# The order of TensorE's work inside a pair of heads, written out as a table: masks, V products and plain score tiles placed anew, VectorE's order with it

## The chip, the cores and the metric

One Trainium2 chip (trn2), one of its cores. The metric is the device time of one execution in microseconds (us): the median of three runs of the kernel before is 3874.01 us (3871.12 to 3876.84).

## The reference, cut to what matters

```python
x = L0_attn_x                                  # (8, 1024, 512) float32
xn = _layernorm(x)
qkv = xn @ W_attn + b_attn                     # q, k, v: 16 heads of 32
att = einsum('bhqd,bhkd->bhqk', q, k) * HD ** (-0.5)
att = where(causal, att, -inf);  att = softmax(att)
y = einsum('bhqk,bhkd->bhqd', att, v) @ W_proj + b_proj
x = x + y + ffn(xn)                            # ffn: SwiGLU, 512 -> 1408 -> 512, FP4-rounded operands
```

The change touches only the softmax attention of the eight batches. Projections and feed-forward stay as they are.

## The kernel before, in words

The kernel works through eight batches, seven in a loop and the last one written out behind it, and then the feed-forward part, 64 tiles of 128 rows. In a batch it projects q, k and v, then goes through the 16 heads in eight **pairs** (`p` = 0 to 7), then multiplies by the output weights. A pair is split into eight **units** `u`, one for each block `kt` of 128 keys.

TensorE does five kinds of work in a pair:

- **Plain score tiles**, `scores(p, n)` (L983): 128 queries against all keys up to them, used only for the row maximum. There are 16 in a pair of heads, n = 0 to 15. Tiles of even n have 640, 768, 896 and 1024 keys and go to the PSUM tile `ps_s`; those of odd n have 512, 384, 256 and 128 keys and go to `ps_dense`. `mask_scores` (L988) adds the causal mask, and VectorE takes the maximum (`row_max`, L609, the tile `mx`). A tile waits until VectorE has read the one two places ahead of it (`s_max`). Tile n stands one or two pairs ahead: the first `EARLY` tiles of pair 1 are made before pair 0 starts; beside pair p stand tiles `EARLY` to 15 of pair p+1, and then, after the maxima of p+1, the tiles 0 to `EARLY`-1 of pair p+2.
- **Maxima**, `maxima(p+1)` (L993): one transposition of all 16 maxima. It needs all 16 `row_max`. VectorE splits the result (`split_max`, L615 and L617), and SP's queue puts it into the stack of operands with two DMAs.
- **Transposed scores**, `transposed_scores(p, kt, i)` (L1010): parts of up to 512 queries; four parts in units 0 to 3 and two in units 4 to 7, 24 in all. They go through a ring of three PSUM banks, `ps_st`: a part waits until ScalarE has taken the exponential (L883) of the part three places ahead. A part on the diagonal gets `mask_transposed` (L1017) before ScalarE may read it.
- **V products**, `times_v(p, kt)` (L1029), four column tiles of 32 side by side: a **visit** here is an uninterrupted run of such narrow products.
- **Denominators**, `denominators(p)` (L1046), also narrow: ones times the sums that GpSimd makes of the exponentials of blocks 0 to 4 (`sum_up`, L536 to L541, tile `stage`), and times the exponentials of blocks 5 to 7 (in `rob`). They are made one pair late, and go to the bank that the odd score tiles use.

From the denominators a chain leads on: VectorE copies them out (`copy_den`, L626), SP's queue spreads them with four small DMAs (`den_rows`, L458), VectorE inverts them (`invert`, L630), SP's queue sends the inverse out and back (L463, L466), and VectorE divides the V product (`divide`, L646).

Every engine's order is fixed by the program. Queues on SP: `den_rows`, the two DMAs of the maxima, the spreading of the inverse, and then, in pairs 1 to 4 of a batch, seven DMAs (L409) that load the q and k of a pair three ahead; these go out as soon as the last exponential of the pair before is done. The storage of the exponentials of block 4 is also that of block 1, so ScalarE may write block 1 of the next pair only once GpSimd has added block 4.

## Time and profile before

| | |
|---|---|
| median of the runs | 3874.01 us |
| profiled execution | 3873.68 us, span of its core 3871.9 us |
| TensorE (PE) busy | 3745.3 us, 97% |
| VectorE (DVE) / ScalarE (ACT) / GpSimd (POOL) busy | 2628.4 / 1212.9 / 932.3 us |
| mean granted TensorE clock | 0.985 |
| attention | eight batches up to about 2320 us of the span, some 281 us each |
| the batch read here | projections from 1161 us, pair 0 at 1244.5, pair 6 at 1371.5, output product 1410.7 to 1442 us |

PE is nearly always busy by the profile, but busy time of pipelined matmuls covers small gaps; what an order costs is read from start to start. In the batch read here the eight pairs begin at 1244.48, 1265.92, 1287.0, 1308.19, 1329.28, 1350.4, 1371.47 and 1390.85 us.

### The profile page before, as it was taken

What the parts mean: (1) busy time and instruction counts of PE and PEld (TensorE: products, weight loads), DVE (VectorE), ACT (ScalarE), POOL (GpSimd) and SP (SyncE); (2) the same over time, 40 slices, a digit from 0 to 9 for tenths busy, and PEclk for the clock granted to TensorE, in tenths of its full rate; (3) what the DMA queues carried; (4) which work ended last, traced back from release to release, by engine and by line L of the source; (5) the groups of instructions that cost most, each with busy time, mean ns of one, the idle gap of its engine ahead of it and who ended that gap; (6) DMA issues with size and microseconds to landing.
All of it is one profiled execution on the core that took longest, in us unless ns stands there. A gap on an engine that the chain in (4) does not pass through costs nothing.

```text
span 3871.9 us, 63727 instructions
## 1 busy us (share of the span) xinstructions
PE 3745.3 (97%) x21836; PEld 2696.1 (70%) x21836; DVE 2628.4 (68%) x3834; ACT 1212.9 (31%) x2313; POOL 932.3 (24%) x462
## 2 busy tenths in 40 slices
PE   8999999999999999999999989999999999999999
PEld 6557556557557556556556548888888888888887
DVE  5665665665665666665666647777777777777777
ACT  2441441441442532532532522222222222222222
POOL 0550550550650641641641630000000000000000
PEclk9999999999999999999999999999999999999999
DMA  5425425426325335335236440111111111111110
GB/s 194 101 73 178 102 73 176 99 73 186 83 88 176 80 105 157 79 118 157 67 117 191 134 164 28 32 31 32 32 32 33 33 33 33 33 33 32 32 31 32
DMA packets 178222, 337.02 MB, mean 87 GB/s; under 512 B 42432, under 2 KB 50112, under 8 KB 176832
## 3 DMA queue, kind: packets, MB, share of 16 engines
q1 hardware_dynamic: 153504, 275.75, 25.1%
q10 hardware_dynamic: 24480, 58.21, 4.4%
q8 instruction: 135, 2.21, 0.3%
q14 instruction: 103, 0.84, 0.1%
HBM read 213.92 MB, written 118.43 MB: 86 GB/s over the span
## 4 chain that ended last, share of the span: by engine, by line
PE 91%; DVE 4%; issue 2%; ACT 1%; DMA 1%; SPq 0%; ACTq 0%; DVEq 0%; POOL 0%
PE f_ps L1471 25%; PE ps_dense L959 13%; PE f_ps_o L1483 12%; PE ps_st L1010 9%; PE ps_s L983 6%; PE ps_dense L1128 5%; PE ps_dense L1029 4%; PE ps_y L1029 4%; PE ps_dense L1046 3%; DVE mx L609 2%; PE ps_st L1017 2%; PE ps_dense L983 2%; PE f_ps L1463 1%; PE ps_s L988 1%; PE ps_st L928 1%
## 5 line engine op out<-in xcount | busy, mean ns | idle before, releaser
L1471 PE MATMUL f_ps<-wgu,xqt 128*128 128x512 f32 (+1 forms) x4608 | 992.6, 373 | 1.4 <-DVE xqt L1331 1.4
L1471 PEld LDWEIGHTS f_ps<-wgu,xqt 128*128 128x128 f32 x4608 | 842.2, 188 | 122.9 <-DVE xqt L1331 1.7
L883 ACT ACTIVATE pt<-ps_st 128x512 f32<-128x512 f32 (+3 forms) x1152 | 551.4, 527 | 656.5 <-PE ps_st L1017 508.5
L609 DVE TENSOR_REDUCE mx<-ps_s 128x1 f32<-128x640 f32 (+3 forms) x576 | 553.7, 961 | 200.6 <-PE ps_s L988 197.6
L541 POOL TENSOR_TENSOR stage<-stage,pt 128x1536 f32<-128x1536 f32 (+2 forms) x176 | 518.4, 2945 | 15.2
L1483 PE MATMUL f_ps_o<-wd,hqt 128*128 128x512 f32 x2112 | 510.9, 394 | 0.6 <-DVE hqt L1357 0.6
L539 POOL TENSOR_TENSOR stage<-pt 128x1792 f32<-128x1792 f32 x64 | 258.3, 4036 | 1012.0 <-ACT pt L883 1012.0
L1483 PEld LDWEIGHTS f_ps_o<-wd,hqt 128*128 128x128 f32 x2112 | 390.9, 188 | 78.9 <-DVE hqt L1357 0.8
L959 PE MATMUL ps_dense<-arena,wa 128*128 128x512 f32 x1536 | 391.7, 402 | 12.9 <-DVE stage L662 7.0
L609 DVE TENSOR_REDUCE mx<-ps_dense 128x1 f32<-128x512 f32 x448 | 219.2, 489 | 217.0 <-PE ps_dense L988 211.9
L959 PEld LDWEIGHTS ps_dense<-arena,wa 128*128 128x128 f32 x1536 | 281.2, 190 | 74.2 <-issue 10.6
L1010 PE MATMUL ps_st<-stack 98*128 98x512 f32 (+3 forms) x768 | 308.3, 425 | 0.2
L1010 PE MATMUL ps_st<-arena 98*128 98x512 f32 (+3 forms) x768 | 282.5, 409 | 3.4 <-ACT pt L883 1.3
L1017 PE MATMUL ps_st<-identb,causal 128*128 128x128 bf16 x1024 | 239.3, 234 | 0.0
L1010 PEld LDWEIGHTS ps_st<-stack 98*128 98x128 f32 x768 | 146.2, 199 | 127.3 <-ACT pt L883 68.6
L1010 PEld LDWEIGHTS ps_st<-arena 98*128 98x128 f32 x768 | 138.9, 190 | 137.2 <-ACT pt L883 75.6
L1128 PE MATMUL ps_dense<-wp,yt 128*128 128x512 f32 x512 | 229.2, 598 | 2.5 <-DVE rob L657 2.0
L1418 ACT ACTIVATE silu<-f_ps 128x512 f32<-128x512 f32 (+1 forms) x192 | 107.0, 557 | 370.5 <-PE f_ps L1471 370.5
L983 PE MATMUL ps_s<-stack 96*128 96x512 f32 (+1 forms) x576 | 181.1, 388 | 35.1 <-DVE mx L609 28.7
L848 ACT ACTIVATE stage<-ps_dense,bqk 128x512 fp32r<-128x512 f32 x128 | 87.5, 687 | 348.8 <-PE ps_dense L959 304.3
L959 PE MATMUL ps_dense<-wa,arena 128*128 128x512 f32 x768 | 189.9, 397 | 0.0
L1413 ACT ACTIVATE ha<-ht 128x1408 f32<-128x1408 f32 x63 | 87.0, 1382 | 325.2 <-DVE ht L1254 325.2
(130 smaller groups left out, 4876.1 us busy)
## 6 DMA issues: line engine op xcount, KB each, us to landing
qk_scratch<-stage SPq DMA_DIRECT2D x128, 512.0 KB, 2.9
stack<-qk_scratch SPq DMA_DIRECT2D x192, 256.0 KB
arena<-qk_scratch SPq DMA_DIRECT2D x192, 256.0 KB
xs<-in_L_attn_x SPq DMA_DIRECT2D x64, 256.0 KB, 3.8
rob<-in_L_attn_x ACTq DMA_DIRECT2D x64, 256.0 KB, 2.8
acc_scratch<-rob ACTq DMA_DIRECT2D x64, 256.0 KB, 2.1
xt<-in_L_attn_x SPq DMA_DIRECT2D x64, 256.0 KB, 2.6
at<-acc_scratch SPq DMA_DIRECT2D x64, 256.0 KB, 2.6
```

What stands on the lines that cost most here:

```text
L539: nc.gpsimd.tensor_tensor(both[:, :, cols], exps(0)[:, :, cols], exps(1), ALU.add).then_inc(summed_up, 1)
L541: nc.gpsimd.tensor_tensor(both[:, :, cols], both[:, :, cols], exps(kt), ALU.add).then_inc(summed_up, 1)
L609: nc.vector.tensor_reduce(mx[:, h * ST + q:h * ST + q + 1], scores_bank(p, n)[:, 0:(q + 1) * P], axis=AX.X, op=ALU.max, negate=True).then_ ...
L883: nc.scalar.activation(exps(kt)[:, h, q - kt * P:q - kt * P + n], ps_st[:, w % ST_RING, 0:n], ACT.Exp, scale=SCALE).then_inc(st_exp, 1)
L959: last = nc.tensor.matmul(bank(*use), left(lh, k), right(rh, k), start=n == 0, stop=n == len(terms) - 1)
L983: nc.tensor.matmul(out[:, k0:k1], qs, stack(p)[0:KS, 2 + h, k0:k1], start=True, stop=k1 < keys)
L1010: last = nc.tensor.matmul(ps_st[:, w % ST_RING, 0:n], stack(p)[0:KM, 2 + h, kt * P:(kt + 1) * P], stack(p)[0:KM, h, q:q + n], start=True, ...
L1017: nc.tensor.matmul(ps_st[:, w % ST_RING, 0:P], causal[:, :], identb[:, :], start=False, stop=True).then_inc(st_full, 1)
L1029: last = nc.tensor.matmul(by_tile(y_bank(p)[y_rows(h, s), y_cols(kt, s)]), v_head(kt, p, h), exps_of_parity(kt, h, s), start=kt == 0, stop ...
L1128: last = nc.tensor.matmul(bank("P", k), yt[:, g, t * P:(t + 1) * P], wp[:, g, :], start=g == 0, stop=g == G - 1)
L1471: last = nc.tensor.matmul(ps[:, SLOT[c], gu, 0:n].rearrange("p (j n) -> p j n", n=P), xqt[:, a, k], wgu[:, b, gu * FC + f // P:gu * FC + ( ...
L1483: last = nc.tensor.matmul(ps_o[:, :], hqt[:, a, k], wd[:, b, k], start=i == 0, stop=i == len(terms) - 1)
```

## The change

`SHARE`, `M_UNIT`, `DEN_UNIT` and `Y_UNIT` go. TensorE's order in a pair is read from a table with a row for each unit: `T` is the next plain score tile, `MT` the masks of all tiles that lack one, `S0` to `S3` the parts of transposed scores, `M0` to `M3` their masks (a `-` names the unit before), `P0` to `P7` the V products, `DEN` the denominators and `MAX` the maxima. VectorE has a table of its own. No instruction is added or removed on any engine but ScalarE's wait registers.

```diff
-    SHARE = [2, 3, 3, 2, 2, 2, 2, 0]
-    M_UNIT = 2
-    EARLY = TILES - sum(SHARE[:M_UNIT + 1])
-    DEN_UNIT = 1
-    Y_UNIT = ST - 1
+    STEPS = ["T MT S0 S1 T MT S2 T S3 MT M2 P5 T M3 MT DEN P6",
+             "S0 S1 S2 T MT T MT M2 S3 T MT M3 P7 P0 MAX",
+             "S0 T S1 S2 T MT M2 P1 T MT S3 M3",
+             "S0 T MT S1 S2 T MT M2 S3 T M3",
+             "S0 M0 MT S1",
+             "S0 T S1 T M1- MT M0 M1 P2 P3",
+             "S0 S1",
+             "S0 T MT M0- M1- M0 P4 S1 M1"]
+    VECTOR_STEPS = "R R R R DEN R R R MAX INV R R R R R R R Y R R"
+    FLAT = " ".join(STEPS).split()
+    EARLY = TILES - FLAT[:FLAT.index("MAX")].count("T")
...
@@ VectorE
-                    if p == PAIRS - 2 and not final and 0 <= u - M_UNIT - 1 < XR:
-                        stats(b + 1, u - M_UNIT - 1)
+                    elif step == "MAX":
+                        if p + 1 < PAIRS:
+                            split_max(p + 1)
+                        if p == PAIRS - 2 and not final:
+                            for t in range(XR):
+                                stats(b + 1, t)
...
@@ ScalarE
+                            act.wait_ge(pv_done, ONE + b * PAIRS * ST + p * ST)
...
@@ TensorE: of a pair
-                    elif 0 < u <= RINGED:
-                        times_v(p, u - 1)
+                        elif step[0] == "P":
+                            kt = int(step[1])
+                            if kt < u:
+                                times_v(p, kt)
+                            elif p:
+                                times_v(p - 1, kt)
```

`EARLY` goes from 8 to 9. P5, P6 and P7 of a pair are made in units 0 and 1 of the next one, P0 in unit 1, P1 in unit 2, P2 and P3 in unit 5, P4 in unit 7. Written in the same letters, the order before was:

```
u0: S0 S1 T S2 M2 MT P5 P6 P7 S3 T M3 MT
u1: S0 S1 T S2 M2 MT DEN P0 S3 T T M3 MT
u2: S0 T S1 T S2 M2 MT P1 S3 T M3 MT
u3: S0 S1 MAX T S2 M2 MT P2 S3 T M3 MT
u4: S0 T M0 MT P3 S1 T M1 MT
u5: S0 T M0 MT P4 S1 T M1 MT
u6: S0 T M0 MT S1 T M1 MT
u7: S0 M0 S1 M1
```

**Place A, TensorE, end of unit 1 and start of unit 2 of a middle pair, before.** The tiles of 896, 256 and 1024 keys (the last three rows on L983) follow each other with two parts between them.

```order
L983 MATMUL ps_s<-arena 128x384
L1017 MATMUL ps_st<-identb,causal 128x128
L988 MATMUL ps_dense<-causal,identb 128x128
L988 MATMUL ps_s<-causal,identb 128x128
L1008 REGISTER_ALU
L1010 MATMUL ps_st<-arena 128x512
L978 REGISTER_ALU
L983 MATMUL ps_dense<-arena 128x256
L1008 REGISTER_ALU
L1010 MATMUL ps_st<-arena 128x512
L978 REGISTER_ALU
L983 MATMUL ps_s<-arena 128x512 x2
```

The same three tile sizes after (now in units 0 and 1; the 896 tile stands ahead of the denominators, so the rows begin with the 256 tile): three parts go ahead of the 256 tile, and it and the 1024 tile have a mask between them.

```order
L1036 MATMUL ps_st<-arena 128x512
L1034 REGISTER_ALU
L1036 MATMUL ps_st<-arena 128x512
L1034 REGISTER_ALU
L1036 MATMUL ps_st<-arena 128x384
L1002 REGISTER_ALU
L1009 MATMUL ps_dense<-arena 128x256
L1014 MATMUL ps_dense<-causal,identb 128x128
L1004 REGISTER_ALU
L1009 MATMUL ps_s<-arena 128x512 x2
L1014 MATMUL ps_s<-causal,identb 128x128
L1043 MATMUL ps_st<-identb,causal 128x128
```

What moved: the tile of 256 keys comes a whole run of narrow products and three parts after the one of 896, which was one part before.

**Place B, TensorE, the denominators of the pair before; before the change.** They stood in unit 1, ahead of P0.

```order
L1017 MATMUL ps_st<-identb,causal 128x128
L988 MATMUL ps_s<-causal,identb 128x128
L1034 REGISTER_ALU
L1036 REGISTER_ALU
L1046 MATMUL ps_dense<-stage,ones 32x512 x4
L1046 MATMUL ps_dense<-rob,ones 32x128 x2
L1046 MATMUL ps_dense<-rob,ones 32x256 x2
L1046 MATMUL ps_dense<-rob,ones 32x128 x6
L1023 REGISTER_ALU
L1029 MATMUL ps_dense<-pt,v 32x512 x4
```

After: they end unit 0, behind the masks of the 896 tile, and P6 follows them.

```order
L1009 MATMUL ps_s<-arena 128x384
L1043 MATMUL ps_st<-identb,causal 128x128
L1014 MATMUL ps_s<-causal,identb 128x128
L1060 REGISTER_ALU
L1063 REGISTER_ALU
L1073 MATMUL ps_dense<-stage,ones 32x512 x4
L1073 MATMUL ps_dense<-rob,ones 32x128 x2
L1073 MATMUL ps_dense<-rob,ones 32x256 x2
L1073 MATMUL ps_dense<-rob,ones 32x128 x6
L1055 MATMUL ps_y<-rob,v 32x128 x4
```

What moved: `denominators` from behind three of unit 1's parts to ahead of all of them, and P6 from unit 0's one run of P5, P6 and P7 to behind it.

**Place C, VectorE, from the maxima on, before.** `inv` was inverted two row maxima after the split of the maxima.

```order
L615 CAST mr<-ps_dense 16x128
L617 TENSOR_TENSOR mr<-ps_dense,mr 16x128
L608 REGISTER_ALU
L609 TENSOR_REDUCE mx<-ps_s 128x1
L608 REGISTER_ALU
L609 TENSOR_REDUCE mx<-ps_dense 128x1
L629 REGISTER_ALU
L630 RECIPROCAL inv<-den 128x16
L608 REGISTER_ALU
```

After: at once behind the split.

```order
L633 REGISTER_ALU
L634 REGISTER_ALU
L635 CAST mr<-ps_dense 16x128
L637 TENSOR_TENSOR mr<-ps_dense,mr 16x128
L649 REGISTER_ALU
L650 RECIPROCAL inv<-den 128x16
L628 REGISTER_ALU
L629 TENSOR_REDUCE mx<-ps_s 128x1
L628 REGISTER_ALU
```

What moved: the reciprocal, past two row maxima. Since MAX itself moves from unit 3 to the end of unit 1, all row maxima of the pair's second half now stand behind the reciprocal.

## Rows read from the trace of the kernel before

**Rows 1.** Stretches: us; busy of PE, PEld, DVE, ACT, POOL; clock, DMA share, GB/s.
```profile
1308.19:1329.28 21.09, 20.39 (x171) 11.84 (x170) 14.46 (x23) 10.71 (x25) 13.26 (x6) 1.00 0.39 86
```

**Rows 2.** PE timeline, pair 3, units 1 and 2: start, us, instruction, idle before.
```profile
1316.38 0.48 PE L1010 MATMUL ps_st<-arena 98*128 98x512 f32 x1
1317.17 0.38 PE L983 MATMUL ps_dense<-stack 96*128 96x256 f32 x1 [0.31 <-DVE mx L609]
1317.39 0.39 PE L1010 MATMUL ps_st<-arena 98*128 98x512 f32 x1
1318.17 0.73 PE L983 MATMUL ps_s<-stack 96*128 96x512 f32 x2 [0.39 <-DVE mx L609]
```

**Rows 3.** PE timeline, pair 3, unit 4, and the passage to pair 4.
```profile
1323.18 0.22 PE L988 MATMUL ps_dense<-causal,identb 128*128 128x128 bf16 x1
1323.21 0.48 PE L1010 MATMUL ps_st<-arena 98*128 98x512 f32 x1
1323.53 0.51 PE L983 MATMUL ps_s<-stack 96*128 96x512 f32 x2
...
1329.08 0.23 PE L1017 MATMUL ps_st<-identb,causal 128*128 128x128 bf16 x1
1329.28 0.74 PE L1010 MATMUL ps_st<-stack 98*128 98x512 f32 x2
```

**Rows 4.** PE timeline, pair 3: denominators with P0, and P1.
```profile
1312.64 1.06 PE L1046 MATMUL ps_dense<-stage,ones 128*32 128x512 f32 x8
...
1315.36 0.44 PE L1010 MATMUL ps_st<-arena 98*128 98x384 f32 x1
...
1319.13 1.06 PE L1029 MATMUL ps_y<-pt,v 128*32 128x384 f32 x8
1320.13 0.38 PE L1010 MATMUL ps_st<-arena 98*128 98x256 f32 x1
```

**Rows 5.** DVE timeline, pair 3: denominators' copy, and the next division.
```profile
1314.69 0.69 DVE L626 COPY rob<-ps_dense 128x512 f32<-128x512 f32 x1 [0.98 <-PE ps_dense L1046]
...
1330.58 1.41 DVE L646 TENSOR_TENSOR yt<-ps_dense,rob 64x512 f32<-64x512 f32 x2 [0.62 <-DMA rob<-inv_scratch]
```

**Rows 6.** SP's issues, pair 3: q and k, denominators, inverse out.
```profile
1308.56 2.67 SPq L409 DMA_DIRECT2D arena<-qk_scratch  x6
...
1315.41 3.54 SPq L458 DMA_DIRECT2D den<-rob  x4
...
1324.32 0.34 SPq L463 DMA_DIRECT2D inv_scratch<-inv  x1
```

**Rows 7.** The tile `den` from 1308 to 1331 us.
```profile
DMA to landing us min/median/max: 1.7/2.6/3.1
```

**Rows 8.** Stretches around the end of the DMA traffic, pair 3.
```profile
1316.50:1318.00 1.50, 1.00 0.12 17
```

**Rows 9.** POOL and PE timelines, pairs 6 and 7.
```profile
1380.61 4.01 POOL L539 TENSOR_TENSOR stage<-pt 128x1792 f32<-128x1792 f32 x1 [7.77 <-ACT pt L883]
...
1385.27 8.93 POOL L541 TENSOR_TENSOR stage<-stage,pt 128x1536 f32<-128x1536 f32 x3
```

**Rows 10.** PE timeline, pairs 6 and 7: their first parts, both runs of denominators.
```profile
1371.47 0.73 PE L1010 MATMUL ps_st<-arena 98*128 98x512 f32 x2
...
1394.55 1.06 PE L1046 MATMUL ps_dense<-stage,ones 128*32 128x512 f32 x8
...
1407.41 0.62 PE L1046 MATMUL ps_s<-stage,ones 128*32 128x512 f32 x2
```

**Rows 11.** PE timeline, start of pair 0.
```profile
1244.48 1.20 PE L1010 MATMUL ps_st<-stack 98*128 98x512 f32 x2
1245.69 0.90 PE L983 MATMUL ps_s<-stack 96*128 96x512 f32 x2
```

**Rows 12.** A stretch of the early tiles of pair 1.
```profile
1242.00:1244.00 2.00, 1.27 (x4) 0.60 (x3) 1.30 (x2) 0.00 (x0) 0.00 (x0) 0.50 1.05 242
```

**Rows 13.** The page, part 5: feed-forward products of 512 columns: busy, mean ns.
```profile
L1471 PE MATMUL f_ps<-wgu,xqt 128*128 128x512 f32 (+1 forms) x4608 | 992.6, 373 | 1.4 <-DVE xqt L1331 1.4
```

More of the change, by code:

```diff
@@ L1078, in body @@
                 mask_scores(1, n)
+            due, unmasked = 0, []
             for p in range(PAIRS):
+                pe.wait_ge(m_in, ONE + b * PAIRS * 2 * DMA + (p + 1) * 2 * DMA)
                 for u in range(ST):
-                    tiles = beside(p, u)
-                    if u == 0:
-                        pe.wait_ge(m_in, ONE + b * PAIRS * 2 * DMA + (p + 1) * 2 * DMA)
-                    parts = len(PARTS[u])
-                    ahead = 2 if u == M_UNIT else 1
-                    for i in range(parts // 2):
-                        transposed_scores(p, u, i)
-                        if u == M_UNIT and i < ahead:
-                            for n in tiles[i:i + 1]:
-                                scores(*n)
@@ L1092, in body @@
-                    if u == M_UNIT + 1 and p + 1 < PAIRS:
-                        maxima(p + 1)
-                    if u != M_UNIT:
-                        for n in tiles[:ahead]:
-                            scores(*n)
-                    if parts > 2:
-                        transposed_scores(p, u, 2)
-                    mask_transposed(p, u, parts - 2)
-                    for n in tiles[:ahead]:
-                        mask_scores(*n)
-                    if u == DEN_UNIT and p:
-                        denominators(p - 1)
@@ L1104, in body @@
-                    if u == 0 and p:
-                        for kt in range(RINGED, ST):
-                            times_v(p - 1, kt)
-                    elif 0 < u <= RINGED:
-                        times_v(p, u - 1)
-                    transposed_scores(p, u, parts - 1)
-                    for n in tiles[ahead:]:
-                        scores(*n)
-                    mask_transposed(p, u, parts - 1)
-                    for n in tiles[ahead:]:
-                        mask_scores(*n)
@@ L1115, in body @@
-            for kt in range(RINGED, ST):
+                    for step in STEPS[u].split():
+                        if step[0] == "S":
+                            transposed_scores(p, u, int(step[1]))
+                        elif step[0] == "P":
[4 more added lines that the diff above has]
+                                times_v(p - 1, kt)
+                        elif step == "T":
+                            tile, due = tile_of(due), due + 1
+                            if tile[0] < PAIRS:
+                                scores(*tile)
+                                unmasked.append(tile)
+                        elif step == "MT":
+                            for tile in unmasked:
+                                mask_scores(*tile)
+                            unmasked = []
+                        elif step == "DEN":
+                            if p:
+                                denominators(p - 1)
+                        elif step == "MAX":
+                            if p + 1 < PAIRS:
+                                maxima(p + 1)
+                        else:
+                            mask_transposed(p, u - step.count("-"), int(step[1]))
@@ L1116, in body @@
+            for kt in PV_LATER:
                 times_v(PAIRS - 1, kt)
```

55 lines of the change are left out of this document (30 added, 25 removed).

## Prediction

> **What bounds the kernel now.** I read the busy shares first, then the pairs' starts, then TensorE's timeline of one middle pair from start to start, then what the other engines do at the same places. Pair 3 lasts 21.09 us, and TensorE is busy in 20.39 of them, at a granted clock of 1.00, 2.4 GHz; VectorE 14.46, ScalarE 10.71, GpSimd 13.26 [rows 1]. So TensorE's own order sets a middle pair, and its two true gaps, 0.31 and 0.39 us, make up the whole of the missing 0.70: both are plain score tiles that wait for VectorE's maximum [rows 2]. GpSimd, though it is busy for 13 us only, sets the passage from pair 6 to pair 7 (below), and the start of pair 0 runs at the lower clock.
>
> What the reader is to see in [rows 2]: the part S0 starts at 1316.38, and the next instruction, a tile of 256 keys, at 1317.17, 0.79 us later. The same succession without a wait takes 0.32 us (1323.21 to 1323.53) [rows 3]. The next part and the tile of 1024 keys behind it take 0.78 us again. Excess: 0.47 + 0.46 = 0.93 us. The tile behind the wait also starts with its weights not yet loaded: 256 columns take 0.22 us there. In an unbroken run a product of up to 512 columns takes 992.6 / 4608 = 0.215 us [rows 13], so 256 take some 0.11; I add 0.2 for both tiles. The waits cost 1.1 us a pair; bounds: the bare gaps, 0.70, and 1.25.
>
> **The change, term by term, for a middle pair.**
>
> *No work goes.* The counts of matmuls, maxima, exponentials and DMAs are the same. The number of visits of narrow products is six before (P5 to P7; DEN with P0; P1; P2; P3; P4) and six after (P5; DEN with P6; P7 with P0; P1; P2 with P3; P4). What entering and leaving one costs is paid six times in both, so the visits give nothing by themselves.
>
> *Waits for maxima, -1.1.* In the order after, I laid the steps out with the distances from start to start of pair 3 and VectorE's durations beside them. Every tile then finds its bank free: the tile of 256 keys comes after DEN, P6 and three parts. DEN takes 2.72 - 1.00 = 1.72 us (denominators with P0, less P1, which is of P0's size) [rows 4], P6 some 0.35, the three parts some 0.75: 2.8 us from DEN's start. It needs the copy of the denominators, which starts 2.05 us after DEN's start (1312.64 to 1314.69) and lasts 0.69 [rows 4, 5]: 2.74 us. It just fits. The 896 tile stands ahead of DEN, so its maximum is long over. I take all 1.1 as gained; if the copy is late, it costs the difference, 0.1.
>
> *End of a pair, -0.17.* From the last mask to the next pair's first part it is 0.20 us, against 0.03 from a mask to a part elsewhere [rows 3]: the part waits for an exponential. After, a tile and its mask stand there first.
>
> *New crossings, +0.2.* Runs of masks followed by a wide product with float32 weights: ten before, eleven after; and the transposition of the maxima, which stood among parts, now comes behind P0 and has to load its weights in the open. Each is 0.1 or a little more (0.32 us for a part of 512 columns behind a mask [rows 3], against 0.215 [rows 13]). Bounds 0 and 0.35.
>
> *VectorE's reciprocal, +0.15 in four pairs.* The new order puts `invert` ahead of nine row maxima. The next in line is the maximum of the 640 tile, on which the 768 tile waits; behind that stands everything in the pair. By my layout, in time since the pair's start: copy done at 6.3; SP issues the four small DMAs, in 3.54 us [rows 6], the last of them some 3 us after the first, and the last landing follows 1.7 to 2.6 us later [rows 7]: about 11.0. VectorE comes to the reciprocal at 10.1, the 640 tile is ready for it at 10.9, and TensorE wants the 768 tile at about 11.9, when reciprocal (0.24) and maximum (0.8) must be over. So a landing by 10.9 costs nothing, one at 11.0 about 0.1 to 0.2. Before, the reciprocal stood 8.7 us behind the copy and never waited here. This matters in pairs 1 to 4, where the q and k of a later pair are loaded at the same time: these go out 0.37 us into the pair (1308.56) [rows 6], and the DMA engines are nearly free from 8.3 us on (1316.50, share 0.12) [rows 8]. The copy was then done at 7.2 us; now it is at 6.3. Bounds: 0 and 1.5.
>
> The Trainium skill has a rule that speaks against the change at this place. In "DMA: Bandwidth & Descriptors", section "Queues, rings and completion order", it says that a DMA's semaphore increment lands only after every earlier write of the same DMA engine. By that rule the small DMAs cannot complete before the loads ahead of them, about 8.5 us into the pair; with the issue time that gives the same 11, and no more, as long as the loads don't last longer. The trace agrees so far: landings up to 3.1 us where the loads were still running, 1.7 where not.
>
> *Division.* From the inverse's first DMA to the division it is 6.26 us (1324.32 to 1330.58), of which VectorE stood 0.62 idle [rows 5, 6]. After, the inverse goes out at about 11.3 (behind the two DMAs of the maxima on SP's queue), so it is there at 17.6; VectorE comes to the division at 17.5 to 17.8, and what waits behind it are maxima of 128 and 640 keys, wanted at 19.9 and 20.8. Cost nothing; cover 1 us.
>
> *GpSimd.* Its sums start with block 1's last exponential and take 13.55 us (1380.61 to 1394.16) [rows 9]. In the new order that start is at 8.4 us into the pair, the end at 22, which is 2 us into the next pair; DEN comes at 3.6. Hidden, with 1.6 us of cover in middle pairs.
>
> Sum for a middle pair: -1.1 - 0.17 + 0.2 = -1.07; six pairs (0 to 5), -6.4; the reciprocal, +0.15 x 4 = +0.6: **-5.8 us**.
>
> **The rest of a batch.**
>
> *Start of pair 0, +1.2.* One tile more is made ahead of it. The tile of 640 keys starts at 1245.69, as soon as VectorE has read the 1024 tile; before, two parts filled the time since 1244.48 [rows 11]. Now nothing fills it: 1.2 us. The granted clock falls to 0.50, 1.2 GHz, in the gaps of the early tiles [rows 12], and pair 0 begins at it. If the return is put off by the same 1.2 us, up to 0.6 more is lost.
>
> *Pair 6, -0.7.* DEN of pair 6 (1394.55) starts 0.4 us after GpSimd's last sum (1394.16), so from pair 6's start, 1371.47, to there GpSimd is the bound: 9.14 us until it begins, 13.55 of sums [rows 9, 10]. What TensorE gains in pair 6 is worth nothing; only that block 1 is ready at 8.4 instead of 9.14 counts.
>
> *Pair 7, +1.3.* From DEN of pair 6 to DEN of pair 7 it is 12.86 us [rows 10]. There are no score tiles left to fill with. After the change all four parts of block 1, and P6 and P7, stand behind DEN of pair 6, where only one part did; ScalarE starts on block 1 some 2.3 us after DEN where it started at once; and units 3 to 5 have no V products between their parts, so TensorE waits for ScalarE's ring there, and then makes P2 and P3 while ScalarE has little. Laid out, DEN of pair 7 comes 14.2 us after that of pair 6; bounds 13.2 and 14.6.
>
> Sum for a batch: -5.8 + 1.2 - 0.7 + 1.3 = **-4.0 us**, eight batches: -32 us. The profiled execution took 3873.68 us, 0.33 below the median of the runs, so the sum holds against either: **3842 us**.
>
> **The rivals.**
>
> *A bigger gain.* Waits at 1.25, crossings at nothing, the reciprocal never late, pair 7 at its lower bound: -1.4 x 6 + 1.2 - 0.7 + 0.35 = -7.6 a batch, 3813 us. For it: the layout has slack nearly everywhere, and TensorE may pull weight loads forward better. Against: ten crossings before became no fewer.
>
> *The small DMAs come late and VectorE holds TensorE up (slower).* Mechanism: the denominators' copy is done 0.9 us earlier in the pair, in the middle of the loads; one issue on SP can then take longer, as one did within the 3.54 us, and landings stretch. Each us of landing past 11 is a us of TensorE, in pairs 1 to 4 of each batch, 32 in all. Above a batch's remaining gain of 4.0 us it turns the sign: landing later than 12.0. With 3.54 us of issue starting late and the 3.1 us landing behind the last it is 12.4 to 12.9, a loss of 1.4 to 1.9 a pair: 3842 + 32 x 1.5 = 3890 us. Against: the longest landing belongs to the DMAs issued first, and the traffic ends at 8.5.
>
> *The change does not do what it says in net.* The edges (early tile, clock, pair 7 at 14.6) eat what the middle gives, 1.8 + 1.7 - 0.7 = 2.8 a batch, and the middle gives only 0.7 - 0.35 + 0.17 = 0.5 a pair: 3874 us, no difference.
>
> *The clock.* The Trainium skill, "TensorE: Matmul & The Clock Gate", section "Why this matters for your kernels", warns of idle gaps between bursts of matmuls, which send the clock back. Where it fell here, TensorE waited after each early tile [rows 12]. If pair 7's waits did the same, the output product of 31 us would run partly at half clock, several us a batch: 3870 or more. The waits there are shorter than a us each, so I give it little; it stands within the case of no difference.
>
> **How the numbers follow.** My sum or near it, 3825 to 3858: 0.62. The bigger gain, below 3825: 0.12. A smaller gain, 3858 to 3866: 0.10. No difference (within 0.2%, 3866 to 3882, about what a measurement can tell): 0.08. Slower, above 3882: 0.08. Faster is 0.62 + 0.12 + 0.10 = 0.84. The range that leaves no more than 2 in 10 out goes from 3814 to 3867.
>
> **What would show it.** Right: a middle pair of 19.9 to 20.2 us with no gap before a tile; the reciprocal within 0.3 us behind the split; first tiles at 1.2 GHz a us longer; DEN to DEN of the last two pairs at about 14.2. Wrong: reciprocals that wait for the small DMAs by more than a us; middle pairs above 20.6; a clock below 1.00 behind pair 7; or the 256 tile waiting for the copy.

## The result, and the profile after

The kernel after takes 3881.52 us (median of 20 runs, 3875.97 to 3889.91), the kernel before 3873.66 us beside it (20 runs, 3869.03 to 3879.25): ratio 1.002, 95% interval 1.0013 to 1.0027. The change made the kernel slower, by 0.2%. The profiled execution has a span of 3880.4 us (before 3871.9), at a mean granted clock of 0.971 (before 0.985). The forecast, 3842 us and faster, was wrong.

The page, part 1 (busy time, share, instructions) and part 4 (the chain that ended last, by engine):

```profile
PE 3755.6 (97%) x21836; PEld 2704.8 (70%) x21836; DVE 2627.6 (68%) x3834; ACT 1217.0 (31%) x2313; POOL 933.6 (24%) x462
PE 89%; DVE 4%; issue 3%; DMA 2%; SPq 1%; POOL 1%; ACT 1%; ACTq 0%; DVEq 0%; POOLq 0%
```

The work is the same and the busy shares tell nothing. The chain does: TensorE's share of it fell from 91% to 89%, and that of DMA rose from 1% to 2%. Of the DMAs, the tile `den` is the one to ask about. The whole kernel's summary of it says that VectorE stood idle before the reciprocal for 74.2 us in 41 places. That sum is no price. 31.4 us of it stand in pair 7 of the first seven batches, one wait of 3.7 to 5.2 us each, and nothing shows that they cost anything: the kernel g1 below has such waits too (some 3.6 us) and takes 12.86 us there, as before the change. Another 21.2 us are short waits of 0.34 to 1.11 us in the middle pairs. In the last batch (2060 to 2300 us) it is this, the times being until a small DMA was there, and from issue to landing:

```profile
  DMA den<-rob: 21.6, 6
DMA to landing us min/median/max: 1.6/4.1/8.0
```

**Where the time went.** The ruler that stands in both orders is the denominators' row of eight products with 512 columns, one per pair. A middle pair, the one of [rows 1], now begins with these steps (PE timeline, start, us, instruction):

```profile
1300.54 1.06 PE L1073 MATMUL ps_dense<-stage,ones 128*32 128x512 f32 x8
...
1303.37 0.36 PE L1009 MATMUL ps_dense<-stack 96*128 96x256 f32 x1
1303.57 0.23 PE L1014 MATMUL ps_dense<-causal,identb 128*128 128x128 bf16 x1
1303.61 0.71 PE L1009 MATMUL ps_s<-stack 96*128 96x512 f32 x2
...
1320.42 1.06 PE L1073 MATMUL ps_dense<-stage,ones 128*32 128x512 f32 x8
```

No row has an idle time behind it, where [rows 2] had 0.31 and 0.39 us. From row to row of this kind it is 19.88 us, where it was about 21.1: -1.23 a pair in this batch. Over the first seven batches the mean is 19.96 against 21.12, -1.16. So the change made the middle pairs shorter, as it was to do, in seven batches. The table sets the two kernels side by side; each number is the distance between two denominators' rows, in us.

| | pairs 1 to 6 (five distances) | to pair 7 | to the last | sum |
|---|---|---|---|---|
| the batch read, before | 21.10, 21.18, 21.11, 21.09, 21.34 | 18.37 | 12.86 | 137.05 |
| the batch read, after | 19.88, 19.88, 19.88, 19.86, 19.85 | 18.55 | 15.56 | 133.46 |
| last batch, before | 21.46, 21.07, 21.06, 21.06, 21.06 | 18.39 | 12.81 | 136.91 |
| last batch, after | 27.26, 27.30, 29.77, 24.19, 19.78 | 18.80 | 15.80 | 162.90 |

The first such row of the last batch comes 17.0 us earlier than before (2106.37 against 2123.36), the last one 9.0 us later (2269.27 against 2260.27), and the feed-forward part begins 8.5 us later (2312.3 against 2303.8), which is the difference of the spans. Seven batches gain 17 us, and the last one loses 26.

**What happens in the last batch.** The pair with the second of the long distances, 27.30 us, begins at 2130.1. Queues of ScalarE and SP, and VectorE's timeline:

```profile
2130.31 0.33 ACTq L1297 DMA_DIRECT2D wgu<-wq_scratch  x1
2130.61 2.78 SPq L429 DMA_DIRECT2D stack<-qk_scratch  x6
2136.40 2.45 SPq L478 DMA_DIRECT2D den<-rob  x4
```

```profile
2139.76 0.28 DVE L637 TENSOR_TENSOR mr<-ps_dense,mr 16x128 fp32r<-16x128 f32 x1
2144.64 0.25 DVE L650 RECIPROCAL inv<-den 128x16 f32<-128x16 f32 x1 [4.60 <-DMA den<-rob]
2144.81 0.76 DVE L629 TENSOR_REDUCE mx<-ps_s 128x1 f32<-128x640 f32 x1
```

In the last batch alone, ScalarE's queue loads a piece of the feed-forward weights (`load_gate_up`, 0.5 to 2.0 MB) at the start of each pair. The stretches show what that does (columns as in [rows 1]):

```profile
2138.00:2140.00 2.00, 2.00 (x17) 1.07 (x15) 1.45 (x4) 0.71 (x3) 1.38 (x1) 1.00 1.03 231
2140.00:2142.00 2.00, 1.77 (x14) 0.53 (x13) 0.04 (x1) 1.20 (x3) 2.00 (x1) 1.00 0.96 202
2142.00:2144.00 2.00, 0.00 (x0) 0.00 (x0) 0.00 (x0) 0.00 (x0) 1.19 (x2) 1.00 0.16 24
2144.00:2146.00 2.00, 0.37 (x1) 0.37 (x2) 1.36 (x3) 0.00 (x0) 0.00 (x0) 0.50 0.05 4
2146.00:2148.00 2.00, 2.00 (x9) 1.18 (x8) 1.12 (x2) 0.51 (x2) 0.28 (x1) 0.50 0.16 49
```

The DMA engines are full until about 2142, 12 us into the pair, where [rows 8] had them nearly free at 8.3. The four small DMAs, 6.3 us into the pair on SP's queue, are all there only 14.5 us into it. VectorE stands before its reciprocal for 4.60 us, and all row maxima stand behind it in program order; TensorE gets nothing for 3.86 us, and works at 0.50, 1.2 GHz, until 2154.1. From denominators to denominators it takes 27.30 us here, 7.4 more than in a middle pair of the same kernel and 6.2 more than before the change.

The pairs of this batch differ in what is loaded beside them, and so give a comparison within one run:

| last batch, after | pair 1 | pair 2 | pair 3 | pair 4 | pair 5 |
|---|---|---|---|---|---|
| weights loaded, MB | 1.3 | 1.3 | 1.8 | 0.5 | 2.0 |
| q and k of a later pair loaded too | yes | yes | yes | yes | no |
| small DMAs, median from issue to landing, us | 6.4 | 6.3 | 7.5 | 4.1 | 1.7 |
| reciprocal's wait, us | 4.55 | 4.60 | 6.14 | 2.11 | none |
| to the next denominators, us | 27.26 | 27.30 | 29.77 | 24.19 | 19.78 |

Pair 5 has the largest piece of weights and no loss. Its traffic is nearly over when its small DMAs go out at 2217.66:

```profile
2217.00:2219.00 2.00, 2.00 (x15) 1.42 (x13) 1.28 (x3) 1.26 (x3) 0.00 (x0) 1.00 0.48 198
DMA to landing us min/median/max: 1.6/1.7/1.7
```

So neither the q and k alone (the other seven batches) nor the weights alone (pair 5) hold the reciprocal up by more than about a us; both together do.

**The ends of a batch.** From the first early tile of pair 1 to the first denominators it was 32.80 us and is 34.23 (1226.55 to 1260.78), although pair 0 no longer waits in its middle; over all eight batches the mean rose by 1.2 us. The stretches in which pair 0 begins:

```profile
1235.00:1237.00 2.00, 2.00 (x7) 1.39 (x8) 1.07 (x3) 0.00 (x0) 0.00 (x0) 0.50 1.03 221
...
1243.00:1245.00 2.00, 2.00 (x12) 1.05 (x14) 1.33 (x3) 0.88 (x2) 0.00 (x0) 0.50 0.00 0
1245.00:1247.00 2.00, 2.00 (x11) 0.55 (x4) 0.33 (x2) 0.13 (x2) 1.82 (x1) 0.67 0.04 8
```

TensorE is busy in all 2.00 us of each, and has 0.50 as its granted clock until 1245 or so; in all the clock was low for 17 us here, against 10 before. (Of the eight batches, two had 14 us before and one had 20 after.) At the other end, the last denominators but one wait for GpSimd, and the clock falls behind them:

```profile
1365.06 4.03 POOL L559 TENSOR_TENSOR stage<-pt 128x1792 f32<-128x1792 f32 x1 [6.18 <-ACT pt L908]
...
1378.68 1.26 PE L1073 MATMUL ps_dense<-stage,ones 128*32 128x512 f32 x8 [1.88 <-POOL stage L561]
...
1394.24 0.62 PE L1073 MATMUL ps_s<-stage,ones 128*32 128x512 f32 x2
```

This end is not the same in every batch. In six of the eight the granted clock falls to 0.50 behind this wait, and from these denominators to the last ones it takes 15.4 to 16.8 us. In the first and the seventh it stays at 1.00, and the same instructions take 14.02 us. The first batch (its denominators, and the stretch behind them), and the stretch of the batch above:

```profile
254.93 1.07 PE L1073 MATMUL ps_dense<-stage,ones 128*32 128x512 f32 x8 [2.10 <-POOL stage L561]
256.00:258.00 2.00, 2.00 (x32) 1.30 (x24) 0.69 (x1) 0.45 (x1) 0.21 (x1) 1.00 0.00 0
1380.00:1382.00 2.00, 2.00 (x28) 1.26 (x20) 0.24 (x1) 0.00 (x0) 0.00 (x0) 0.50 0.00 0
```

The mean of the seven batches is 15.3 us, 2.45 more than before the change.

### The profile page after: what moved, and what is told of

It is laid out like the page before. It is cut to its first block, busy times and chain, and to the rows that moved or that the text cites. A ratio compares the mean times of both kernels' runs of the same rounds, so it can differ in the third digit from the quotient of the medians.

```text
span 3880.4 us, 63776 instructions
## 1 busy us (share of the span) xinstructions
PE 3755.6 (97%) x21836; PEld 2704.8 (70%) x21836; DVE 2627.6 (68%) x3834; ACT 1217.0 (31%) x2313; POOL 933.6 (24%) x462
## 4 chain that ended last, share of the span: by engine, by line
PE 89%; DVE 4%; issue 3%; DMA 2%; SPq 1%; POOL 1%; ACT 1%; ACTq 0%; DVEq 0%; POOLq 0%
PE f_ps L1492 25%; PE ps_dense L984 13%; PE f_ps_o L1504 12%; PE ps_st L1036 8%; PE ps_s L1009 7%; PE ps_dense L1149 4%; PE ps_y L1055 4%; PE ps_dense L1055 3%; PE ps_dense L1073 3%; PE ps_dense L1009 2%; PE ps_st L1043 1%; PE f_ps L1484 1%; DMA den<-rob 1%; DVE mx L629 1%; PE ps_s L1014 1%
## 5 line engine op out<-in xcount | busy, mean ns | idle before, releaser
L908 ACT ACTIVATE pt<-ps_st 128x512 f32<-128x512 f32 (+3 forms) x1152 | 568.6, 526 | 649.7 <-PE ps_st L1036 378.0
L984 PEld LDWEIGHTS ps_dense<-arena,wa 128*128 128x128 f32 x1536 | 280.0, 190 | 72.6 <-issue 10.7
L1036 PE MATMUL ps_st<-stack 98*128 98x512 f32 (+3 forms) x768 | 271.3, 416 | 0.0
L1036 PE MATMUL ps_st<-arena 98*128 98x512 f32 (+3 forms) x768 | 253.1, 400 | 9.8 <-ACT pt L908 6.5
L1009 PE MATMUL ps_s<-stack 96*128 96x512 f32 (+1 forms) x576 | 195.8, 415 | 43.1 <-DVE mx L629 36.7
L1043 PE MATMUL ps_st<-identb,causal 128*128 128x128 bf16 x1024 | 199.4, 230 | 0.0
L1371 DVE TENSOR_TENSOR h<-silu,f_ps 128x512 f32<-128x512 f32 (+1 forms) x192 | 122.5, 638 | 97.1 <-ACT silu L1439 97.1
```

What stands on the lines that cost most here:

```text
L908: nc.scalar.activation(exps(kt)[:, h, q - kt * P:q - kt * P + n], ps_st[:, w % ST_RING, 0:n], ACT.Exp, scale=SCALE).then_inc(st_exp, 1)
L984: last = nc.tensor.matmul(bank(*use), left(lh, k), right(rh, k), start=n == 0, stop=n == len(terms) - 1)
L1009: nc.tensor.matmul(out[:, k0:k1], qs, stack(p)[0:KS, 2 + h, k0:k1], start=True, stop=k1 < keys)
L1036: last = nc.tensor.matmul(ps_st[:, w % ST_RING, 0:n], stack(p)[0:KM, 2 + h, kt * P:(kt + 1) * P], stack(p)[0:KM, h, q:q + n], start=True, ...
L1043: nc.tensor.matmul(ps_st[:, w % ST_RING, 0:P], causal[:, :], identb[:, :], start=False, stop=True).then_inc(st_full, 1)
```

## The experiments

My theory (A): in the last batch the reciprocal, moved ahead of the maxima, waits for small DMAs that are held up by the weight loads. Its rival (B): the weight loads hold up the loads of q and k that the score tiles need, and the reciprocal only waits along; then VectorE's order would not matter. A third reading, for e3: the new order costs more in the last batch by itself, or the clock does, whatever is loaded. The start and the end of a batch are terms apart.

**e1: the reciprocal two row maxima later, as before.**

```diff
-    VECTOR_STEPS = "R R R R DEN R R R MAX INV R R R R R R R Y R R"
+    VECTOR_STEPS = "R R R R DEN R R R MAX R R INV R R R R R Y R R"
```

> The changed kernel with VectorE's reciprocal of the denominators two row maxima later (MAX R R INV ...), as far behind the split as it stood before the change. Theory A: the changed kernel loses its gain in the last batch alone, where the four small DMAs of the denominators land late beside the large loads of the feed-forward weights, the reciprocal waits for them on VectorE with all row maxima behind it, and TensorE waits and then runs at 1.2 GHz. From denominators to denominators the last batch's pairs take 27.3, 27.3, 29.8 and 24.2 us against 19.9 in the others: 29 us. With two maxima ahead of the reciprocal, only the third score tile behind it is held up, by some 1.5 us instead of 5, and the clock should mostly hold: pairs of 21 to 22.5 us, 3860 us in all (3853 to 3866). Theory B: the large loads hold up the loads of q and k for the score tiles themselves, and the reciprocal only waits along: then this changes nothing, 3878 to 3885 us.

Measured: 3861.69 us, 0.9967 of before (0.9955 to 0.9978). The last batch has 23.65, 21.90, 26.09 and 20.17 us in place of 27.26, 27.30, 29.77 and 24.19; a middle pair keeps 19.86. One place in VectorE's order is worth 20 us and turns the sign of the whole change. The total is as expected, though two of the pairs lie above the 22.5 us that I had given as their bound: the reciprocal still waits there, 2.52 and 3.78 us.

**e2: the reciprocal far back, and the division a pair later.**

```diff
+    VECTOR_STEPS = "R Y R R R DEN R R R MAX R R R R INV R R R R R"
...
-                    elif p and p < PAIRS - 1:
-                        divide(p - 1)
+                    elif p > 1:
+                        divide(p - 2)
```

> The changed kernel with the reciprocal four row maxima behind the split, and the division moved from the end of a pair to behind the first row maximum of the next one (R Y R R R DEN R R R MAX R R R R INV R R R R R). Theory A: no wait for the small DMAs is left, pairs of the last batch take 19.9 to 20.5 us; 3881.5 - 29 = 3852 us (3848 to 3857). Theory B: pairs of the last batch stay at 24 to 30 us, 3878 to 3885 us.

Measured: 3891.15 us, 1.0043 (1.0029 to 1.0056), above what either theory gave. The point in dispute can be read all the same: in the four slow pairs the reciprocal's waits of 4.55, 4.60, 6.14 and 2.11 us became 0.84, 0, 0.93 and 0, and the last batch's pairs take 20.6 to 21.3 us, with the denominators and the loads where they were, hardly more than this kernel's middle pairs in the other batches. That excludes B, by which they stay at 24 to 30 us. But the middle pairs of the seven other batches rose to 20.7 to 20.8, and the kernel got slower. The reason stands on VectorE in each pair:

```profile
1314.85 0.69 DVE L629 TENSOR_REDUCE mx<-ps_dense 128x1 f32<-128x512 f32 x1 [0.60 <-PE ps_dense L1014]
1315.57 1.41 DVE L666 TENSOR_TENSOR yt<-ps_y,rob 64x512 f32<-64x512 f32 x2
1317.01 0.96 DVE L629 TENSOR_REDUCE mx<-ps_s 128x1 f32<-128x768 f32 x1
```

The division, 1.41 us, now stands ahead of the maximum of the 768 tile, and TensorE wants that bank back. I had put it there because VectorE had idle time in the pair; it has none at that place, and TensorE stands idle for 0.87 us before a later score tile.

**e3: the weight loads later in the pair, behind its fifth block; VectorE's order as changed.**

```diff
-                if final:
-                    shared.load_gate_up(act, p)
                 for kt in range(ST):
+                    if final and kt == RINGED:
+                        shared.load_gate_up(act, p)
```

> The changed kernel with the large load of feed-forward weights of each pair of the last batch issued at key block 5 (some 17 us into the pair) instead of at its start; order of TensorE and VectorE as in the changed kernel. Both theories expect the small DMAs to land in time and the pairs of the last batch at 19.9 to 20.5 us: 3852 us (3848 to 3858). If the loss were the new order's own in the last batch (its registers, its wait for the first weights), or the clock's by itself, 3875 us or more.

Measured: 3856.59 us, 0.9952 (0.9939 to 0.9966). The last batch: 20.0, 24.51, 20.46, 20.56, 19.78 us. This is the other half of the proof: the same reciprocal at the same place, without the weight loads at the head of the pair, and 25 us less. The third reading falls with it. In the one pair that stays long, pair 2, the piece issued late in pair 1 (2117.96) and the q and k keep the DMA engines full until 2130, the small DMAs go out at 2127.68, and the reciprocal still waits:

```profile
2133.91 0.25 DVE L650 RECIPROCAL inv<-den 128x16 f32<-128x16 f32 x1 [2.59 <-DMA den<-rob]
```

**g4: the kernel before, with the reciprocal directly behind the split of the maxima.** It asks whether the reciprocal's new neighbour alone costs anything in the old order.

```diff
                     if u == M_UNIT + 1 and p + 1 < PAIRS:
                         split_max(p + 1)
+                    if u == M_UNIT + 1 and p:
+                        invert(p - 1)
                     for n in tiles[:1]:
...
-                    if u == M_UNIT + 1 and p:
-                        invert(p - 1)
```

> The kernel before with one edit: the reciprocal directly behind the split of the maxima, as the change has it, with everything else at its old place. Theory: what hurts is not that it stands ahead of the row maxima but when the split comes: before, 13.9 us into the pair, when even the late DMAs of the last batch (landed some 14 us into the pair) are nearly there. So 3874 us within 0.1%, and at most 1 us a pair in the last batch. Rival: a reciprocal with a DMA's wait ahead of the row maxima costs wherever it stands: 3880 us or more.

Measured: 3876.72 us, 1.0006 (0.9997 to 1.0015); the last batch has 21.06 to 21.10 and one pair of 22.17. In the old order the split came some 14 us into the pair, in the new one 10. So the reciprocal directly behind the split is harmful only since the maxima come four us earlier: the landing stayed where the loads put it, and what waits for it moved ahead.

**e5: pairs 6 and 7 in the old distribution.** A second table is read for `p` = 6 and 7; pair 7's units 1 to 3 show its kind.

```diff
+    END_STEPS = [STEPS[:3] + [...],
+                 ["S0 S1 S2 M2 P5 P6 P7 S3 M3", "S0 S1 S2 M2 DEN P0 S3 M3", "S0 S1 S2 M2 P1 S3 M3",
...
+                    for step in (STEPS if p < PAIRS - 2 else END_STEPS[p - PAIRS + 2])[u].split():
```

> The changed kernel with other tables for the last two pairs of each batch: pair 6 as changed up to unit 2, then P2, P3, P4 in units 3, 4, 5 between the parts, as before the change; pair 7 with P5 to P7 of pair 6 in unit 0 and the denominators of pair 6 in unit 1 behind three parts, as before the change. Theory: of the 15.6 us between the denominators of the last two pairs (12.9 before the change), the 2.7 us more are lost because ScalarE starts block 1 late and the V products no longer fill its time: 13.0 us again, and 8 x 2.6 = 21 us less in all: 3861 us (3857 to 3868). Rival: GpSimd's sums, which the passage from pair 6 to 7 hangs on, and the wait of 1.9 us for them that lowers the clock are what costs, and stay: then at most 8 us less, 3873 us or more.

Measured: 3862.1 us, 0.9969 (0.9959 to 0.998). From the last denominators but one to the last it is 12.87 us again, in place of 15.56, and their wait for GpSimd is 0.34 in place of 1.88. The last batch's pairs stay at 27.46, 27.24, 29.62 and 24.57: this is another term. The run takes away the wait for ScalarE's ring and the fall of the clock together; what divides the two is the pair of batches of the changed kernel whose clock did not fall (14.02 us).

**g1: e1, e3 and e5 together.**

> Three edits to the changed kernel at once: the reciprocal two row maxima later, the large loads of the last batch at key block 5, and the other tables for the last two pairs. If they act on different places, they add: last batch pairs of 19.9 to 20.2 us throughout (the one of 24.5 that is left with the loads moved goes too), 12.9 us between the last two runs of denominators: 3856.6 - 8 x 2.6 - 5 = 3831 us (3827 to 3838). Rival: both repairs of the last batch mend the same 25 us, and the loads at block 5 then hit the division or the end tables: 3840 or more.

Measured: 3832.91 us, 0.9894 (0.9879 to 0.9909). As expected (3827 to 3838), the three add. The pairs take 19.87 us in the middle batches, 19.78 to 19.79 in the last, and the end 12.86 and 12.81. With the reciprocal never waiting in pairs 1 to 6, no middle pair is longer than 19.89.

**g5: the ninth early tile made in unit 0 of pair 0 instead of ahead of it; all else as changed.**

```diff
-            for n in range(EARLY):
+            for n in range(EARLY - 1):
...
+    FIRST_STEPS = "S0 S1 TE MT T MT T MT S2 T S3 MT M2 T M3 MT"
```

> The changed kernel with one tile moved at the start of each batch: eight early tiles as before the change, the ninth behind the first two parts of transposed scores of pair 0, so that TensorE has work while VectorE reads the tile of 1024 keys. From the first early tile to the first denominators the changed kernel takes 34.2 us (32.8 before the change, although pair 0 lost its two waits). Theory: the ninth tile costs the 1.2 us without work and keeps the clock at 1.2 GHz longer (16 us against 10): 31.5 us with the edit, 8 x 2.7 = 22 us less, 3860 us (3855 to 3867). Rival: only the 1.2 us without work come back: 33.0 us, 3872 us.

Measured: 3879.36 us, 1.0015 (1.0006 to 1.0024), which the intervals don't tell from the changed kernel (1.0013 to 1.0027), and neither theory's number. At the place itself the rival's number came out. From the first early tile to the first denominators it is 32.91 us in the batch read (rival 33.0, theory 31.5), and 33.3 in the mean of the eight, against 34.5 in the changed kernel and 33.2 before. The stretch at 1.2 GHz did not go back to the 10 us of before, but it is 14 us in five of the batches, where it was 17 or more, and those five have the shortest starts (32.9 to 33.1 us). So the ninth tile ahead of pair 0 accounts for about 1.1 us a batch. The whole kernel shows only 2 of these 9 us: the long pairs of the last batch took 2 us more than in the changed kernel, and the rest is not accounted for. With the repairs in, the same move gave 5.7 us (g6 against g1).

**g8: the V product P0 of pair 0 early, the rest as changed.** In the traces until then the clock had come back within P0 of pair 0, so I tried P0 earlier: unit 1 `S0 P0 S1 S2 ...`, unit 2 `S0 MAX T ...`, in pair 0 alone.

> The changed kernel with another order in pair 0 alone: P0 as the second step of unit 1 instead of next to last, and the maxima behind unit 2's first part. In the kernel before, the changed kernel and the one with the ninth tile moved, the granted clock came back from 0.50 to 1.00 within the run of P0's products of pair 0, 7.4, 11.4 and 11.3 us after the last longer gap. Theory: it is P0's products that bring it back, and the changed kernel pays for having P0 late in unit 1. With P0 some 3 us earlier the clock is at 1.00 some 3.5 us earlier: 1.5 to 1.8 us a batch, 3867 us (3862 to 3872). Rival: the clock comes back when it does, whatever is issued: 3881 us.

Measured: 3883.79 us, 1.0031 (1.002 to 1.0043). P0 stood at 1236.40, and the low clock ended within its products: the coincidence held a fourth time. The low stretch was 14 us in seven of the eight batches, 3 us shorter than in the changed kernel, as the theory had it. The time did not fall, as its rival had it: from the first early tile to the first denominators it takes 34.7 us in the mean (34.5 in the changed kernel). The transposition of the maxima now waited for VectorE in this order:

```profile
1236.40 1.64 PE L1056 MATMUL ps_dense<-pt,v 128*32 128x512 f32 x8
...
1240.95 0.33 PE L1020 MATMUL ps_dense<-ident,mx 128*128 128x128 f32 x1 [0.74 <-DVE mx L630]
```

**g6: g1 and g5; g7: g6 and g8.**

> The three repairs together (3833 us measured) and the ninth tile in pair 0. If they add: 3833 - 22 = 3811 us by the theory of the run before, 3823 us by its rival.

> The kernel with all repairs (3827 us) and the same order in pair 0. Theory: 3814 us (3809 to 3820). Rival: 3827 us.

Measured: g6 3827.17 us, 0.9877 (0.9862 to 0.9892), the fastest of all and faster than both kernels, but not the 3811 or 3823 us expected; g7 3841.7 us, 0.9914 (0.9901 to 0.9927), above both of its numbers. In g7's profiled execution one batch had its low clock from 384 to 415 us, 31 us on end, and no order explains why this batch and not its neighbours.

**g2: the plain tiles spread anew, V products, denominators and reciprocal at their old places.** It was to say which part of the table gives the middle pair's gain.

```diff
+    STEPS = ["S0 S1 T S2 M2 MT P5 P6 P7 S3 T M3 MT",
+             "S0 S1 T S2 M2 MT DEN P0 T MT S3 T M3 MT",
+             "S0 S1 T S2 M2 MT P1 T MT S3 T M3 MT",
+             "S0 S1 S2 M2 P2 MAX T MT S3 T M3 MT",
...
```

> One part of the change alone: the V products, denominators and reciprocal at their old places (P5 to P7 in unit 0, DEN with P0, P1, P2, P3, P4 in units 1 to 5, reciprocal two maxima behind the split, eight early tiles), only the score tiles are spaced so that none of 256 or 1024 keys stands one or two parts behind another, and each is masked at once. Theory: what a middle pair gains (21.1 to 19.9 us) are the two waits for maxima and the one for an exponential at the pair's end; the spacing alone gives the two waits: 20.1 to 20.4 us a pair, nothing lost at the start of a batch, in pair 7 or in the last batch: 6 x 8 x 0.9 = 43 us, 3831 us (3822 to 3845). Rival: the gain comes from where the V products and the masks stand: 20.8 us or more a pair, 3860 us or more.

Measured: 3858.83 us, 0.9959 (0.9945 to 0.9973), and a pair of 20.86 us: only 0.25 of the 1.23 gained. That is the rival's number (20.8 or more), not the theory's (20.1 to 20.4). Both waits of [rows 2] are gone in this order, and one of its own, behind the split, stands in their place:

```profile
1309.77 0.49 PE L1009 MATMUL ps_dense<-stack 96*128 96x512 f32 x1 [0.29 <-DVE mr L637]
```

The new gap of 0.29 us does not fill the 0.85 us that are missing. So removing the two waits does not by itself give the 1.1 us that I had put down for them; the places of the V products, the masks and the denominators have a large share, and no run here divides it further. It loses nothing in the last batch (20.8 us a pair), and so is faster than the whole change by 23 us, with the lesser middle.

**g3: the changed order, but the masks of the plain tiles behind the V products beside them.**

```diff
-    STEPS = ["T MT S0 S1 T MT S2 T S3 MT M2 P5 T M3 MT DEN P6",
-             "S0 S1 S2 T MT T MT M2 S3 T MT M3 P7 P0 MAX",
+    STEPS = ["T MT S0 S1 T MT S2 T S3 P5 MT M2 T M3 MT DEN P6",
+             "S0 S1 S2 T MT T MT M2 S3 T MT P7 P0 M3 MAX",
...
```

> The changed kernel with the masks of transposed scores and of score tiles put behind the V products again, wherever a visit stood directly behind masks (P5, P7 with P0, P1, P2, P4). Theory: masks ahead of V products only give ScalarE and VectorE their input earlier by the 0.6 to 1.2 us that a visit takes; for ScalarE, busy 10.7 of 20 us, that buys nothing, for VectorE it does where the next tile of the same bank follows the visit: the tile behind P1 then waits about 0.7 us, the one behind P5 0.3. Middle pairs 20.6 to 21.2 us; 3915 us (3900 to 3935), about the gain of the middle lost. Rival: it makes no difference, 19.9 us a pair, 3880 us.

Measured: 3984.03 us, 1.0282 (1.0268 to 1.0296), three times the loss that I had expected: a middle pair of 21.85 us (expected 20.6 to 21.2), 2.0 more than in the changed kernel, with a wait of 0.81 us for a maximum and one of 0.36 for an exponential:

```profile
1301.93 0.62 PE L1009 MATMUL ps_s<-arena 96*128 96x512 f32 x2 [0.81 <-DVE mx L629]
```

A tile's maximum can't start before its mask, so a mask behind a V product delays VectorE by the whole product. The two waits are 1.17 of the 2.0 us. Of the parts of the table that were taken out here, "masks ahead of V products" is the dearest.

## Why the prediction was wrong

**Right in size: the middle pair.** Forecast -1.07, measured -1.23 in the batch read and -1.16 in the mean of seven. The two waits of [rows 2] are gone. The tile of 256 keys just fits behind the copy of the denominators, as laid out (2.74 us against 2.8): the copy, 0.69 us, began at 1302.59, and the tile starts at 1303.37. The gap of a pair's end went too. How the gain divides is not shown: the sum gives the waits 1.1 us and everything else next to nothing, but g2, without these waits, has only 0.25. That the total agrees is in part luck.

**Right: pair 6.** GpSimd starts at 8.48 us into pair 6 (forecast 8.4), and the last denominators but one come at 22.1 (forecast 22), where they came at 23.08: -1.0 for the -0.7 forecast. (From denominators to denominators it is +0.18, only because those that open the distance now stand earlier in the pair.)

**Wrong, and the step that failed: "VectorE's reciprocal, +0.15 in four pairs".** It reckons that the small DMAs are there about 11.0 us into the pair, because "the DMA engines are nearly free from 8.3 us on". That was read from pair 3 of a middle batch [rows 6 to 8] and taken for all eight batches. It is right for seven: there the landing came 10.7 us into the pair read. A wait of up to some 0.7 us did not lengthen a pair (19.86 to 19.88), and a longer one did by about the rest of it (1.04 us: 20.24; 1.11 us: 20.31), 0.12 a pair in the mean, beside the +0.15 of the sum. In the last batch the weight loads on ScalarE's queue and the loads of q and k keep the engines full until 12 us, and the DMAs land 14.5 us into the pair. The four pairs take 108.5 us where four of 19.87 would take 79.5: the term is +29 us in this batch, not +0.6. e1 and e3 each take most of it away, from the two sides (VectorE's order, the loads), and e2 takes away nearly all of the wait. The data was there to be read: in the last batch of the kernel before, the tile `den` has this row, beside the 1.7/2.6/3.1 of [rows 7]:

```profile
DMA to landing us min/median/max: 1.6/3.1/7.0
```

The 7.0 was harmless there, since the reciprocal stood 8.7 us behind the copy. The change took this cover, and I priced it by the stage where it was not needed.

Every us of wait was also dearer than a us: 4.60 us on VectorE became 7.4 us of pair, because the clock fell with the pause. I had carried that effect only in the case of the output product, not in this one. The rows bear an estimate: after the pause TensorE worked from 2145.63 to 2154.1 at 0.50, which costs at most half of 8.5 us, 4.2; with the pause of 3.86 that is 8.1, near the 7.4.

**The rival that decided.** Its mechanism was the one on record, small DMAs that come late and hold VectorE up, and its turning point too ("landing later than 12.0"). Its place and price were not: 1.5 us in 32 pairs was forecast, and it was 4 to 10 us in four pairs of the last batch, with waits of 2.1 to 6.1 us. The reason given against it, that "the traffic ends at 8.5", was the sentence that did not hold there. The Trainium skill, "DMA: Bandwidth & Descriptors", section "Queues, rings and completion order", makes the increment of a DMA wait for all earlier writes of its DMA engine. The trace agrees with it: the landing of the same small DMAs is 1.7 us with free engines, and up to 8.0 behind the weights, q and k. It does not prove the rule, since small DMAs that merely share full engines would be late too, and no run here tells the two apart. Either way, what the forecast lacked is a list of all loads that are ahead in each stage, the other queues' too.

**Mis-sized: the start of pair 0, +1.2.** The sum from the first early tile to the first denominators grew by 1.43 us in the batch read (1.2 in the mean), near the +1.2 by luck. In it, pair 0 gained its two waits (1.1 by my sum), and the denominators stand 0.9 us earlier in the pair (3.55 against 4.45), so the start itself costs about 1.4 + 1.1 + 0.9 = 3.4 us. The row shows 7 us more at 1.2 GHz, where I had allowed 1.2. g5 puts the ninth tile back into pair 0 and gets 1.1 us back, with a low stretch of 14 us in most batches in place of 17: that is the part of the tile. What the other 2 us are, and what brings the clock back at this place, stays open: P0 stood beside the return in four traces, and g8 and g7, which had it earlier, did not gain by it.

**Mis-sized: pair 7, +1.3.** It was +2.7 in the batch read (15.56 against 12.86), above the bound of 14.6, and +2.45 in the mean. The laid-out part, TensorE waiting for ScalarE's ring, was right: where the clock stayed at 1.00, in two of eight batches, it took 14.02 us against the 14.2 forecast. What was missing is the clock at 0.50 behind the wait of 1.9 to 2.1 us for GpSimd, another 1.3 to 2.8 us in the other six. That is the case that I had as a rival and gave little, because the waits are shorter than a us each. This one is longer. And the early tiles of the kernel before had spoken against the reason already: these are TensorE's waits there, none as long as 0.8 us, before the clock stood at 0.50 in [rows 12].

```profile
1237.56 0.56 PE L983 MATMUL ps_s<-stack 96*128 96x512 f32 x2 [0.78 <-DVE v L669]
1239.11 0.62 PE L983 MATMUL ps_s<-stack 96*128 96x512 f32 x2 [0.56 <-DVE mx L609]
1240.85 0.85 PE L983 MATMUL ps_s<-stack 96*128 96x512 f32 x2 [0.63 <-DVE mx L609]
```

The price was also another than I feared: the low stretch lay in pair 7, and the output product ran at 1.00.

**The sum.** In the mean of seven batches the measured terms are, by the same rulers, -5.8 for five middle pairs, +0.2 to pair 7, +2.45 behind it and +1.2 at the start, -2.0 us a batch in place of -4.0. From the first denominators of a batch to those of the next it is -2.4; the difference lies in the projections and products between. Seven of them alone would have made the kernel faster; the last one turned the sign.

## What to carry to other kernels

An instruction that waits for a DMA must be placed by the worst landing over all stages in which its line runs, not by a typical one: look at the minimum, median and maximum of its landing in every stage, the last batch above all, where the next part's weights come in. On an engine that works in program order the cheapest instruction (0.25 us here) is as dear as everything behind it, and moving other work ahead takes away its cover without touching it. A table of order for the middle of a loop should have rows of its own for the first and the last rounds; here that was worth 19 us.

## What the hardware showed that I had not expected

The clock's loss is not in proportion to the pause. In the last batch TensorE stood idle for 1.37, 3.81, 3.86 and 5.39 us before a score tile, and the pairs in which it did were 4.3, 7.4, 7.4 and 9.9 us longer than 19.87. So 2.9, 3.6, 3.6 and 4.5 us came on top of the pause, while the granted clock was 0.50 for some 7, 10, 10 and 14 us.

The same pause in the same order is not always followed by the lower clock: in pair 7 the wait of 1.9 to 2.1 us was followed by 0.50 in six batches and by 1.00 in two, which is a difference of 1.3 to 2.8 us between batches of one program.

At a batch's start the clock stayed at 0.50 for 17 us with TensorE busy in every us of the last ten, where it was low for 10 in the kernel before. Summed up to the end of the attention part, what is missing to the full clock is 56 us before and 111 us after. The sum is a hint where to look and no measure of time: g6 still has 73 us of it, 17 more than the kernel before, and is 46 us faster.
